# Attention and gated feed-forward on one core: one half turn a unit moved to ScalarE and GpSimd, maxima transposed by a DMA, one gather moved up in SyncE's queue

## The reference, cut to what matters

```python
def proj(w, b):                       # x: (2, 1024, 128), 16 heads of 8
    return (einsum('bld,ed->ble', x, w) + b).reshape(B, L, H, Dh).transpose(0, 2, 1, 3)
q, k, v = proj(wq, bq), proj(wk, bk), proj(wv, bv)
attn = softmax(einsum('bhqd,bhkd->bhqk', q, k) / sqrt(16), axis=-1)
x = layernorm(x + einsum('bld,ed->ble', heads_joined(attn @ v), wo) + bo)
h = silu(lin(x, w1) * s1) * (lin(x, w2) * s2)            # hidden width 512
h = gelu(lin(h, h1) * s)
h = gelu(lin(h, h2) * s)
x = layernorm(x + lin(h, w3) * s3)
```

## Time and profile before

| | us |
|---|---|
| median of the runs | 441.21 |
| profiled execution | 441.35 |
| its span (first to last instruction) | 439.6 |
| TensorE matmul busy | 426.9 |
| VectorE busy | 383.8 |
| ScalarE busy | 363.6 |
| GpSimd busy | 106.9 |

### The profile page before, as it was taken

The page is one execution under the profiler, slowest core; times in us unless marked ns, Lnnn a source line. Parts: engine busy times, 40 slices in busy tenths (PEclk is TensorE's granted clock), DMA queues, the critical chain, the costliest instruction groups (busy, mean ns, idle before and its releaser), DMA issues.

```text
span 439.6 us, 9789 instructions
## 1 busy us (share of the span) xinstructions
PE 426.9 (97%) x3498; PEld 228.3 (52%) x3498; DVE 383.8 (87%) x704; ACT 363.6 (83%) x683; POOL 106.9 (24%) x198
## 2 busy tenths in 40 slices
PE   8999999999999999999999999999999899999995
PEld 3544545444444444444445454544333588877884
DVE  6799999999999999999999999999874576657636
ACT  4497989999998999998899998998799885678762
POOL 9730110101011010101101013958111363046103
PEclk9999999999999999999999999999999999999999
DMA  5667741111131111113011111121021000000101
GB/s 161 174 204 119 281 147 28 49 28 28 48 123 25 40 37 28 28 48 123 25 40 39 26 28 49 16 41 52 10 41 49 15 8 1 1 1 3 48 1 48
DMA packets 17117, 24.89 MB, mean 57 GB/s; under 512 B 5168, under 2 KB 9008, under 8 KB 16688
## 3 DMA queue, kind: packets, MB, share of 16 engines
q1 hardware_dynamic: 16464, 23.68, 19.8%
q10 hardware_dynamic: 608, 0.59, 0.5%
HBM read 15.08 MB, written 7.60 MB: 52 GB/s over the span
## 4 chain that ended last, share of the span: by engine, by line
PE 74%; DVE 12%; ACT 4%; SPq 3%; issue 2%; DMA 2%; POOL 1%; POOLq 0%; DVEq 0%; ACTq 0%
PE ps L1366 23%; PE ps L1288 18%; PE ps L1476 16%; DVE negmax L983 11%; PE ps L1350 9%; ACT arena L663 2%; DMA parts_q<-arena 2%; PE ps L1220 2%; PE ps L1231 1%; PE ps L1420 1%; PE ps L1316 1%; PE ps L1260 1%; SPq L462 1%; SPq L434 1%; ACT v_pad L716 1%
## 5 line engine op out<-in xcount | busy, mean ns | idle before, releaser
L983 DVE TENSOR_REDUCE negmax<-ps 128x1 f32<-128x512 f32 x458 | 274.5, 683 | 1.4 <-PE ps L1288 1.3
L663 ACT ACTIVATE arena<-ps 128x512 f32<-128x512 f32 x360 | 190.3, 605 | 21.3 <-PE ps L1350 14.7
L1350 PE MATMUL ps<-qx,kx 64*128 64x512 f32 x512 | 170.0, 450 | 0.9 <-DMA qx<-mT 0.6
L1288 PE MATMUL ps<-kx,qx 61*128 61x512 f32 x468 | 159.3, 440 | 0.8 <-DMA qx<-parts_q 0.5
L1288 PEld LDWEIGHTS ps<-kx,qx 61*128 61x128 f32 x468 | 75.1, 184 | 86.7 <-DVE negmax L983 76.6
L1366 PE MATMUL ps<-arena,v_pad 128*32 128x256 f32 (+3 forms) x1328 | 104.7, 407 | 2.4 <-ACT arena L663 2.4
L663 ACT ACTIVATE hf<-ps 128x512 f32<-128x512 f32 x152 | 83.3, 602 | 9.5 <-PE ps L1350 8.0
L1350 PEld LDWEIGHTS ps<-qx,kx 64*128 64x128 f32 x512 | 78.6, 184 | 18.2 <-ACT arena L663 11.5
L1476 PE MATMUL ps<-hid,w_high 128*128 128x512 f32 (+1 forms) x296 | 68.3, 387 | 0.8 <-issue 0.4
L1476 PEld LDWEIGHTS ps<-hid,w_high 128*128 128x128 f32 x296 | 54.2, 188 | 12.4 <-issue 0.8
L1366 PE MATMUL ps<-hf,v_pad 128*32 128x128 f32 (+1 forms) x600 | 47.5, 388 | 0.0
(11 more groups left out here) (109 smaller groups left out, 333.7 us busy)
## 6 DMA issues: line engine op xcount, KB each, us to landing
qx<-parts_q SPq DMA_DIRECT2D x60, 64.0 KB, 2.1
late_sb<-in_late SPq DMA_DIRECT2D x3, 1280.0 KB, 5.7
kx<-parts_k SPq DMA_DIRECT2D x56, 64.0 KB, 2.1
parts_q<-prt SPq DMA_DIRECT2D x3, 512.0 KB, 6.4
parts_q<-arena SPq DMA_DIRECT2D x3, 512.0 KB, 8.2
xT_sb<-in_xT SPq DMA_DIRECT2D x4, 256.0 KB, 4.0
xT_sb<-arena SPq DMA_DIRECT2D x28, 32.0 KB
prt<-den SPq DMA_DIRECT2D x7, 128.0 KB
```

The lines of the kernel that those rows point to most:

```text
L663: nc.scalar.activation(probs(n // HG)[:, heads(n), :], ps[:, PLAN["score", n][0], :], ACT.Exp, scale=SCALE).then_inc(exp_done, 1)
L983: nc.vector.tensor_reduce(negmax[:, t // TURNS % 2, m % 2, h * QT + q:h * QT + q + 1], ps[:, MAX_BANK + m % 4, :], AX.X, ALU.max, negate=T ...
L1288: nc.tensor.matmul(ps[:, half_bank(m), :], qx[at, slot, qc, h, q * P:(q + 1) * P], kx[at, slot, h, part * C:(part + 1) * C], start=True, s ...
L1350: nc.tensor.matmul(ps[:, bank, :], kx[at, slot, h % PAIR, kt * P:(kt + 1) * P], qx[at, slot, qc, h % PAIR, :], start=True, stop=True)\
```

## The change

For units 2 to 15, one half (`BESIDE_HALVES`: the first from 32u + 8 on that is the last of its group) is left out on VectorE. ScalarE copies its bank, negated, to SBUF, and GpSimd brings 512 columns to one by a tree of nine levels of three instructions each. The maxima's parts of units 1 to 15 are transposed by a DMA on SyncE's queue into `mT_half`, and GpSimd casts them into `mT`; unit 0 keeps the old way. In the loop the transpose stands ahead of the slot's key loads. `gather(0)` and `move(0)` stand ahead of unit 13's maxima. GpSimd's work is ordered by unit, with two weight slices in each of units 10 to 14 and one in 15, and the residual's bias behind unit 15. The loops on SyncE and VectorE are written out. PE's transposes and ScalarE's copies of the maxima for units 1 to 15 are gone, with their places in the bank rotation.

```diff
+def copied_halves():
+    halves = []
+    for u in range(2, U_ALL):
+        m = 2 * TURNS * u + BESIDE_FROM        # BESIDE_FROM = 8
+        while (m - AHEAD) % RUN != RUN - 1:
+            m += 1
+        halves.append(m)
+    return halves
...
+            def turn_max(i, w):                # SyncE
+                sp.wait_ge(max_split, i * PER + w + 1)
+                sp.dma_start_transpose(mT_half[:, w % 2, :], mpart[:, w % 2, :]).then_inc(max_across[w % 2], 16)
+            def turn_and_load_max(i, w):
+                turn_max(i, w)
+                load_max(i, w)
...
+            turn_max(0, 1)
             sp.dma_start(bo_bc[:], bo.partition_broadcast(P)).then_inc(in_mid, 16)
+            load_max(0, 1)
...
-            with sp.Fori(0, ITERS - 1) as i:
-                load_max(i, 1)
+            for i in range(ITERS - 1):
+                if i > 0:
+                    turn_and_load_max(i, 1)
                 ...
                     load_q(g, slot, 0)
+                    turn_max(i, 2 * slot + 2)
                     sp.wait_ge(scores, base + KT * HG * 3 // 2)
                     load_k(g, slot, 0, C, rows_in[slot][0])
                     load_max(i, 2 * slot + 2)
                     ...
                     if slot == 0:
-                        load_max(i, 3)
+                        turn_and_load_max(i, 3)
...
-            load_max(ITERS - 1, 1)
             gather(0)
             move(0)
-            load_max(ITERS - 1, 2)
+            turn_and_load_max(ITERS - 1, 1)
             spread(0)
-            load_max(ITERS - 1, 3)
+            turn_and_load_max(ITERS - 1, 2)
+            turn_and_load_max(ITERS - 1, 3)
             gather(1)
...
+            def copy_beside(n):                # ScalarE, behind the last exp of the half's group
+                m = BESIDE_HALVES[n]
+                act.wait_ge(max_scores, m + 1)
+                if n > 0:
+                    act.wait_ge(beside_step, BESIDE_STEPS * n)
+                nc.scalar.activation(beside[:], ps[:, half_bank(m), :], ACT.Copy, scale=-1.0)\
+                   .then_inc(beside_out, 1)
...
+            def take_beside(u):                # GpSimd
+                n = u - 2
+                m, done = BESIDE_HALVES[n], BESIDE_STEPS * n
+                h, q = head_of(m // 2)
+                pool.wait_ge(beside_out, n + 1)
+                width = C // 2
+                while width:
+                    a, b = beside[:, 0:width], beside[:, width:2 * width]
+                    out = a if width > 1 else negmax[:, u % 2, m % 2, h * QT + q:h * QT + q + 1]
+                    nc.gpsimd.tensor_tensor(a, a, b, ALU.subtract).then_inc(beside_step, 1)
+                    pool.wait_ge(beside_step, done + 1)
+                    nc.gpsimd.tensor_scalar(a, a, 0.0, None, ALU.min).then_inc(beside_step, 1)
+                    pool.wait_ge(beside_step, done + 2)
+                    nc.gpsimd.tensor_tensor(out, a, b, ALU.add).then_inc(beside_step, 1)
+                    pool.wait_ge(beside_step, done + 3)
+                    done += 3
+                    width //= 2
+            def widen_max(w):
+                pool.wait_ge(max_across[w % 2], 16 * ((w + 1) // 2))
+                if w > 1:
+                    pool.wait_ge(mrow_in[w % 2], MROW_INC * (w // 2))
+                nc.gpsimd.tensor_copy(mT[:, w % 2, :], mT_half[:, w % 2, :]).then_inc(max_copied, 1)
+            def turn_maxima(u):
+                if u >= 2:
+                    take_beside(u)
+                if u >= W_UNIT:                # W_UNIT = 10
+                    halve_w(2 * (u - W_UNIT))
+                g = u // QC + 1
+                if u % QC == 1 and 2 <= g < G_ALL:
+                    pool.wait_ge(pv_done, (g - 1) * QC * KT)
+                    stage_v(g, g % 2)
+                split_max(u)
+                widen_max(u)
+                if W_UNIT <= u < U_ALL - 1:
+                    halve_w(2 * (u - W_UNIT) + 1)
...
+                elif m - 4 in BESIDE_HALVES:   # PE, before a half takes that bank again
+                    pe.wait_ge(beside_out, BESIDE_HALVES.index(m - 4) + 1)
```

More of the change, by code:

```diff
@@ L68 @@
 FOLD = 5
+BESIDE_FROM = 8
+W_UNIT = 10
 TURN_AFTER, COPY_AFTER = 5, 6
@@ L89 @@
 GROUPS_ALL = RUNS + STEPS_ALL - (TAIL - 1)
-TURN_AT = {min((2 * TURNS * (w + 1) - 1 - AHEAD) // RUN + 3, RUNS + 1): w for w in range(1, U_ALL)}
+def copied_halves():
[6 more added lines that the diff above has]
+    return halves
 def heads(n):
@@ L146, in bank_plan @@
             place(("score", n))
-        if g in TURN_AT and g >= RUNS:
-            place(("max", TURN_AT[g]))
         w = unit_from(g)
@@ L161, with taken @@
 PLAN = bank_plan()
+BESIDE_HALVES = copied_halves()
+def taken(m):
+    return m - sum(n < m for n in BESIDE_HALVES)
+BESIDE_STEPS = 3 * (C.bit_length() - 1)
 WO_BANK, X1T_BANK, INEXACT_BANK = [2, 3, 6, 7], [2, 3, 6, 7], 2
@@ L339, in build @@
         max_turned = sem("max_turned")
+        max_across = [sem(f"max_across{s}") for s in range(2)]
         max_copied = sem("max_copied")
@@ L688, in _ @@
                 if t == TURNS + COPY_AFTER:
-                    copy_max(0)
+                    copy_first_max()
             for g in range(-RUN_BEFORE, GROUPS_ALL):
-                if g in TURN_AT and g < RUNS:
-                    copy_max(TURN_AT[g])
                 if g > RUNS and unit_to(g - 1) is not None:
@@ L698, in _ @@
                     exp(n)
+                    if n == scores_of(g)[-1]:
+                        for m in turn_halves(g):
+                            if m in BESIDE_HALVES:
+                                copy_beside(BESIDE_HALVES.index(m))
                     if g >= RUNS and n % HG == 1:
@@ L806, in stage_v, with split_max @@
                 ).then_inc(v_staged, 1)
-            def split_max(i, w):
-                first = i is None
-                i = 0 if first else i
+            def split_max(w):
                 m, rest = (t.rearrange("p (r n) -> p r n", r=2)
-                           for t in (negmax[:, 0, 0, :] if first else negmin[:, w % 2, :], mrest[:]))
+                           for t in (negmax[:, 0, 0, :] if w == 0 else negmin[:, w % 2, :], mrest[:]))
                 none = zeros[:, :].rearrange("p (r n) -> p r n", r=2)
                 parts = mpart[:, w % 2, 0:PARTS * TURNS].rearrange("p (r i n) -> p i r n", r=2, i=PARTS)
[L816 to L823, removed]
+                done, merged = 3 * w, 3 * (w - 1)
+                pool.wait_ge(max_taken, taken((w + 1) * 2 * TURNS))
+                if w > 0:
                     nc.gpsimd.tensor_tensor(mrest[:], negmax[:, w % 2, 1, :], negmax[:, w % 2, 0, :], ALU.subtract)\
@@ L895, in left_gate @@
                                             ALU.subtract).then_inc(gate_ready, 1)
[L898 to L907, removed]
+            for u in range(1, U_ALL):
+                turn_maxima(u)
+            pool.wait_ge(in_mid, 32)
+            nc.gpsimd.tensor_tensor(xres[:], xres[:], bo_bc[:, :].unsqueeze(1).broadcast_to([P, TOK // P, D]),
+                                    ALU.add).then_inc(xres_ready, 1)
             for c in (0, 1):
@@ L1001, in turn_halves_from @@
                     turn_half(i, m)
-            with dve.Fori(0, ITERS - 1) as i:
+            for i in range(ITERS - 1):
                 turn_halves_from(i, 2 * WHOLE, 2 * WHOLE + 2 * PER * TURNS)
@@ L1330, in bank_free, with turn_first_max @@
                 else:
[L1331 to L1338, removed]
+                    pe.wait_ge(max_taken, taken(n))
+            def turn_first_max():
+                pe.wait_ge(max_split, 1)
+                nc.tensor.transpose(first_turned, mpart[:, 0, :], ident_bf[:]).then_inc(max_turned, 1)
             def score(n):
```

48 lines of the change are left out of this document (18 added, 30 removed).

## The result

Six runs of the changed kernel took 448.67 to 451.19 us (median 450.53), six of the kernel before beside them 440.68 to 442.07 (441.51): ratio 1.0199 [1.0175, 1.0223]. The forecast was 443.3, its range ended at 448.5. The profiled executions, on which all sums here are made, took 449.33 (span 447.6) and 441.35 (span 439.6): +7.98 where +2.0 was forecast. The medians are 9.0 us apart; the 1.0 more is in no trace here and stays unexplained.

The account below looks back on a forecast made before the run. VectorE's half turns were taken to set the pace, TensorE and ScalarE within 5%. The units' gain of -4.5 and GpSimd's late chain of +6.5 made +2.0 us on 441.35: 443.3 us, range 437.5 to 448.5.

Parts of the forecast that it names:

- (a): 14 halves leaving VectorE make a unit 0.41 us shorter, about 18.73 us: -4.5 us over some 11 units, bounds -6.6 and 0.
- (b): GpSimd's tree of 27 dependent instructions takes 10.5 us a half, bounds 9 and 12; hidden in units 2 to 9.
- (c): Maxima's way from split to scores: transposing DMA 2.2 us (bounds 1.8 and 5), cast and signal 0.4; costs nothing.
- (e): GpSimd's chain with two weight slices a unit becomes the bound in the last units, delaying the first output projection: +6.5 us.
- R3: Rival: the transposing DMA is slow and lies twice on the path; at 5 us +5.6, 448.9 us; chance 0.13.
- (d): Gather and move ahead of unit 13's maxima in SyncE's queue: about 4 us lost on TensorE, alone +1.3 at the projection.
- (f): Unrolled loops, other banks and the residual's bias moved behind unit 15's cast (4.63 us): nothing.
- R1: Rival: trees under 7.9 us, GpSimd not late, the unit's gain survives: -3.2, 438.1 us; chance 0.25.
- R2: Rival: gain and loss cancel, with a tree 0.5 us shorter and 0.5 gained a unit: 441.35 us; chance 0.20.

Follow-up runs that it names:

- e12: e10 with the 14 halves neither copied by ScalarE nor reduced by GpSimd or VectorE, so that part of the maxima is left out: 437.12 us, 0.9899.
- e1: Changed kernel with unit 13's maxima put back ahead of the first batch's gather and move in SyncE's queue: 449.46 us, ratio 1.0181.
- e3: Changed kernel with the edits of both e1 and e2: 445.30 us, ratio 1.0097.
- e4: e3 with VectorE reducing all halves again, without ScalarE's copies and GpSimd's trees; turning by DMA stays: 447.02 us, ratio 1.0136.
- e2: Changed kernel with GpSimd's weight slices spread out, one in each of units 4 to 14, SyncE's queue as changed: 444.73 us, ratio 1.0093.
- e10: Changed kernel with the edits of both e9 and e2: 439.65 us, ratio 0.9965.
- e9: Changed kernel with SyncE's earlier order: unit 13's maxima, gather and move, unit 14's maxima, broadcasts, unit 15's maxima: 445.85 us, 1.0099.
- e7: Changed kernel with 24 matmuls of unused result in TensorE's 5.4 us wait ahead of the first output projection: 449.53 us, ratio 1.0185.
- e6: Changed kernel without VectorE's wait for the split of unit 15 ahead of its first normalization: 451.39 us, ratio 1.0229.

## Why the prediction was wrong

The direction, the places and the order of the waits came out as written; the size did not, by three terms and one that was missing.

(a) **The gain was too large, and this failed first.** The step set TensorE's unit at 18.53 us from groups of 1.70 and 0.40 at a unit's end, the latter from one pair of rows, and took the larger of two engines' paces (18.54 and 18.53) as the pace of both. e12 shows a unit of 18.77 without any copy, 0.23 above either. Why is not shown: VectorE waits only 0.6 us for TensorE in e12's nine units, but its reductions start 0.602 us apart (93 in a row in 56.09 us) and not 0.598, so its idle time alone doesn't show what a unit costs. The copy itself, put at 0.20, measured 0.19. The unit's gain is 0.17 us instead of 0.41; where 384 scores are done that made 2.45 us instead of 4.5. The bound of 0 to 0.60 held it; the value chosen did not. (That the three engines are "within 5%" doesn't follow from the step's own rows either: ScalarE's 1.55 us a group is 13% below VectorE's 1.79.)

(b) The tree takes 11.0 us on the path of the changed kernel (285.97 to 296.94 in unit 14) rather than 10.5: the minimum against a constant (L889) costs 0.85 us on 256 elements, more than the 0.72 of the subtraction (L887), where some 0.44 follows from the slope that was read off a cast.

```profile
285.97 0.72 POOL L887 TENSOR_TENSOR z<-z 128x256 f32<-128x256 f32 x1
286.78 0.85 POOL L889 TENSOR_SCALAR z<-z 128x256 f32<-128x256 f32 x1
...
296.94 0.61 POOL L924 CAST w_high<-late_sb 128x512 fp32r<-128x512 f32 x1
```

Two trees on the path make the 0.88 us of the table. The count and the place were right.

(c) 2.2 us from issue to landing is what the transposing DMA takes at the median, but the one on the path of (e) took 3.9 in this execution. R3 named the mechanism, twice on the path; it came once, at its price of 1.7 us. Had the forecast asked what stands ahead of each transpose in SyncE's queue it would also have seen the broadcasts, which cost e1, e3 and e4 their gain.

(d) The stall of 3.5 us at score 416 is there, released by the DMA of the maxima. The part of the step by which "some of it comes back" is wrong: e2 against e10 wins nothing back in 28 us, since e10's groups run at TensorE's free pace too, and it loses another 0.8 us in the two groups behind the stall, with the granted clock at 0.93 and 0.89 in the 10 us on either side of 290 (1.00 in the kernel before). That the order's cost is not added to (e) was right for the changed kernel, where the projection waits for GpSimd alone, since the chain of (e) already began at the late cast.

(e) The chain of GpSimd, its idle-free stretch, and the projection's wait for it came as forecast, 4.65 us later by the terms of (a), (b) and (c). e9 and e2 take its two causes, the queue and the slices, away one at a time, and e10 both.

**The missing term** is TensorE's clock: the forecast wrote "What follows the first projection keeps its lengths". It did not; after a wait of 5.4 us the stretch was 1.5 us longer, all of it in the first 3.55 us, at a granted clock of 0.54, and e7, by filling the wait, got the 1.5 back in the profile.

(f) The bias behind unit 15's cast stayed hidden, though it took 5.59 us in place of 4.63. Of the rivals R1 and R2 needed a shorter tree, which no run shows; e10 comes to R1's side of the kernel before only by moving the slices and the loads.

What stays open is why unit 14's transpose took 3.9 us. From its issue to its landing the DMA records of the changed kernel (queue, packets, MB, share) hold one packet of another queue, a load of instructions:

```profile
q1 hardware_dynamic: 160, 0.03, 4.4%
q8 instruction: 1, 0.02, 1.5%
```

A like packet stands beside e9's transposes of 3.8 and 2.8 us, and none beside unit 14's of 2.2 us in e6, e7 and e10. SyncE's instructions in e6 and e7 are those of the changed kernel; there such a packet follows right behind the landing. It coincides, and it changes from one execution to the next; no run takes it away.

## What to carry to other kernels

Where two engines are within a few per cent of each other, the work that one sheds buys about half of its time here (4.7 us of 8.4), and the copy that carries it away half of that again: measure the next engine's pace by leaving the work out, before building the way around it. Work given to an idle engine stands in that engine's order: ask of every wait ahead of it, and of every transfer ahead of that wait, what comes late behind it. A long wait on TensorE cost its length and then a slower stretch behind it: 1.5 us after one of 5.4.

## What was not expected of the hardware

- GpSimd's minimum against a constant is dearer than its two-input subtraction: 0.85 us against 0.73 at 128 x 256, 0.53 against 0.46 at 128 x 128.
- A transposing DMA of 128 x 128 holds SyncE's queue for 1.13 us, a plain one there for 0.42 (L595, ahead of the broadcasts). Behind the four broadcasts it took 6.2 us and more from issue to the load of its rows (e1, e3, e4), 2.6 where nothing was in its way.
- VectorE's flags and folds, which work on SBUF alone, and GpSimd slow each other: in the changed kernel five folds took 7.7 us rather than 3.5 and the bias 5.59 rather than 4.63, off the path; in e6 a slice's subtraction took 2.6 times as long, on it. The Trainium skill ("SBUF — State Buffer", Who interferes with whom) describes a pair of ports that the two engines share, and names it as the only cause of contention in SBUF; the rows agree that both engines slow, and no run here tells the port from another cause.
